# A macaron block (experts, linear attention, experts): attention walked batch by batch, with the norms of the other batch between its units

## What is computed

```python
x = x + 0.5 * _L0_ffn_ref(_layernorm(x), gate_w, Wg, Wu, Wd, cWg, cWu, cWd)
x = x + _L0_attn_ref(_layernorm(x), wq, wk, wv, wo)
x = x + 0.5 * _L0_ffn_ref(_layernorm(x), gate_w, Wg, Wu, Wd, cWg, cWu, cWd)

# attention: q, k rotated (rope); per head, with lam = 2 ** (-8 i / 16):
#   o[i] = sum over j <= i of exp(-lam (i - j)) (q[i] . k[j]) v[j];  result = o @ wo.T
# ffn: logits = x @ gate_w.T; the 4 largest, softmax weights over them;
#   each chosen expert e: down_e(silu(g) * u), plus 0.05 * the chunk expert e // 2
```

## Time and profile before

| | us |
|---|---|
| median of 3 runs | 596.48 (592.13 to 601.65) |
| the profiled execution, its own time | 596.83 |
| its span | 595.1 |
| stage B, from the load of results to the first projection | 153.2 to 181.7 |
| first projections to the first scores | 181.7 to 189.7 |
| stage C, units 0 to 31 | 189.7 to 424.5 |
| stage D to the routing's first matmul | 424.5 to 437.2 |
| routing to the first expert matmul | 437.2 to 458.5 |

### The profile page before, as it was taken

One profiled execution on the slowest core, in us unless ns is written; L12 is line 12 of the kernel. 1 busy time (PEld: TensorE's weight loads), 2 busy tenths in 40 slices (PEclk: granted clock), 3 DMA queues, 4 the chain that ended last, 5 costly groups with the idle time before them and its releaser, 6 DMA issues.

```text
span 595.1 us, 9863 instructions
## 1 busy us (share of the span) xinstructions
PE 507.6 (85%) x3276; PEld 439.8 (74%) x3276; DVE 318.7 (54%) x997; ACT 142.8 (24%) x382; POOL 257.4 (43%) x280
## 2 busy tenths in 40 slices
PE   8589979999039999999999999999858999999900
PEld 7489968887017888889888988888758898888600
DVE  6844333343296647664766476666785444444325
ACT  4102212222234231222132212211420222222211
POOL 0045656663236444434443444333103566666322
PEclk9789999999559999999999999999976999999955
DMA  7989987781650010121012011110295425778173
GB/s 228 322 261 330 331 319 245 257 287 55 236 192 18 28 36 19 54 56 23 31 40 68 19 36 36 52 37 10 86 381 179 154 94 182 234 251 281 55 256 118
DMA packets 46654, 87.79 MB, mean 148 GB/s; under 512 B 6528, under 2 KB 27264, under 8 KB 46592
## 3 DMA queue, kind: packets, MB, share of 16 engines
q1 hardware_dynamic: 37376, 66.05, 34.0%
q0 software_dynamic: 6912, 18.88, 9.4%
q10 hardware_dynamic: 2304, 2.10, 1.0%
HBM read 74.42 MB, written 12.58 MB: 146 GB/s over the span
## 4 chain that ended last, share of the span: by engine, by line
PE 60%; DVE 22%; DMA 11%; issue 3%; SPq 2%; ACT 1%; POOL 1%; POOLq 0%; DVEq 0%; ACTq 0%
PE bank L1180 10%; PE bank L1089 8%; PE bank L1084 7%; PE bank L1217 6%; DMA w_down_sb<-w_down 4%; PE bank L1108 4%; PE bank L1110 4%; PE bank L1193 4%; DVE shared L921 3%; DVE shared L922 3%; DVE shared L920 3%; DMA shared<-z_dram 3%; PE bank L1214 3%; PE bank L1171 3%; PE bank L1199 2%
## 5 line engine op out<-in xcount | busy, mean ns | idle before, releaser
L458 POOL DMA_INDIRECT decay_all<-xn_dram,ids x72 | 69.6, 966 | 121.0 <-PE bank L1056 52.8
L526 POOL TENSOR_TENSOR shared<-shared 128x512 f32<-128x512 f32 x36 | 45.8, 1273 | 130.2 <-DVE shared L922 130.2
L860 DVE COPY oT_all<-bank 128x256 f32<-128x256 f32 x72 | 30.6, 425 | 131.0 <-PE bank L1056 131.0
L467 POOL DMA_INDIRECT z_dram<-probs_all,dest x72 | 70.2, 975 | 36.4 <-ACT probs_all L642 32.7
L1180 PE MATMUL bank<-split_sb 128*128 128x512 f32 x240 | 65.2, 407 | 1.9 <-ACT split_sb L601 0.9
L1089 PE MATMUL bank<-w_ch_sb,oT_all 128*128 128x256 f32 x256 | 65.7, 379 | 0.0
L941 DVE TENSOR_TENSOR split_sb<-bank,split_sb 128x512 fp32r<-128x512 f32 x32 | 22.1, 692 | 66.2 <-ACT split_sb L690 66.2
L634 ACT ACTIVATE rot<-bank 128x224 f32<-128x224 f32 x72 | 25.7, 357 | 132.2 <-PE bank L1089 132.2
L1084 PE MATMUL bank<-w_exp_sb,oT_all 128*128 128x192 f32 x256 | 53.4, 331 | 2.9 <-issue 1.6
L1231 PE MATMUL bank<-split_sb 128*128 128x256 f32 x384 | 53.4, 288 | 1.5 <-DVE split_sb L941 1.5
L1084 PEld LDWEIGHTS bank<-w_exp_sb,oT_all 128*128 128x128 f32 x256 | 43.8, 189 | 10.3 <-issue 5.5
(11 more groups left out here) (141 smaller groups left out, 971.3 us busy)
## 6 DMA issues: line engine op xcount, KB each, us to landing
shared<-w_up_piece SPq DMA_DIRECT2D x32, 448.0 KB, 6.3
w_exp_sb<-w_exp SPq DMA_DIRECT2D x32, 384.0 KB, 8.3
shared<-w_down_piece SPq DMA_DIRECT2D x32, 256.0 KB, 4.3
w_ch_sb<-w_ch SPq DMA_DIRECT2D x16, 384.0 KB, 5.9
shared<-z_dram SPq DMA_DIRECT2D x12, 512.0 KB, 7.1
decay_all<-decay SPq DMA_DIRECT2D x16, 256.0 KB, 2.7
w_down_sb<-w_down SPq DMA_DIRECT2D x16, 192.0 KB, 7.8
xn_dram<-xn_sb ACTq DMA_DIRECT2D x16, 128.0 KB, 6.1
```

The costliest lines, as they stand in the source:

```text
L458: pool.indirect_dma_start(out=xg[s], out_offset=None, in_=xn_dram[l][:, :], in_offset=bass.IndirectOffsetOnAxis(ap=ids[:, SEQ[t]:SEQ[t] + ...
L467: pool.indirect_dma_start(out=z_dram[l][:, :], out_offset=bass.IndirectOffsetOnAxis(ap=dest[:, SEQ[t]:SEQ[t] + 1], axis=0), in_=y_sb[s], i ...
L526: nc.gpsimd.tensor_tensor(dst, rope_a[r % 2], rope_b[r % 2], ALU.add).then_inc(roped, 1)
```

## The change

Attention goes batch by batch: unit n is head n % 16, batch n // 16, so each weight of a head (q, o, decay; k and v of a group) is loaded and split once per batch instead of once for both. The first batch needs only four normalised tiles, so stage B handles tiles 0 to 3. Tiles 4 to 7 are combined on DVE alone (`late_sum`, four chained operations, without ACT and POOL), normalised, transposed and split between units 1 and 11; their residual goes into PSUM in units 12 and 13. In units 17 to 29 the first batch's finished sum is copied out, normalised, transposed, and its logits and top 4 are taken. Stage D then has tiles 4 to 7 alone, and `members` for the first four tiles runs ahead of them.

```diff
-        UNITS, GU = H * B, GROUPS * B
+        UNITS, GS = H * B, HKV * B
         def projections(n, place):
-            g, m = n // GU, n % GU
+            G, m = n // GROUPS, n % GROUPS
             if n < 0:
-                return [("q", 0, 0), ("k", 0, 0), ("v", 0, 0), ("v", 0, 1), ("k", 0, 1), ("t", 0, 0)]
+                return [("v", 0), ("q", 0), ("k", 0), ("t", 0)]
             if place == "scores":
-                return [("q", n + 1, (n + 1) % B)] if n + 1 < UNITS else []
-            if g + 1 < HKV and m >= 2:
-                return [("vvkktt"[m - 2], g + 1, m % 2)]
-            return [("t", 0, 1)] if n == 0 else []
+                return [("q", n + 1)] if n + 1 < UNITS else []
+            return [("vkt"[m - 1], G + 1)] if m >= 1 and G + 1 < GS else []
...
         def splits(n):
             if n < 0:
-                return [("q", 0), ("k", 0)]
-            found = [("o", n // 2)] if n % 2 == 0 else [("q", (n + 3) // 2)] if n + 3 < UNITS else []
-            if n == 0:
-                found.append(("q", 1))
-            if n % GU == 3 and n // GU + 1 < HKV:
-                found.append(("k", n // GU + 1))
+                return [("q", 0), ("k", 0), ("q", 1)]
+            found = [("o", n)]
+            if n + 2 < UNITS:
+                found.append(("q", n + 2))
+            if n % GROUPS == 1 and n // GROUPS + 1 < GS:
+                found.append(("k", n // GROUPS + 1))
...
+        LATE_SUM_AT, LATE_STATS_AT, LATE_NORM_AT, LATE_TURN_AT, LATE_COPY_AT, LATE_RES_AT = 1, 2, 3, 4, 5, 12
+        OUT_AT, STATS_AT, NORM_AT, TURN_AT, COPY_AT, LOGIT_AT, TOP_AT = [H + a for a in (1, 2, 3, 4, 5, 6, 7)]
+        def early_tile(n, first):
+            i = (n - first) // 2
+            return [i] if (n - first) % 2 == 0 and 0 <= i < SB else []
...
+        def load_late(sp, j):
+            if j == 1:
+                sp.wait_ge(xnT_mm, TT + SB)
+            if j >= 2:
+                sp.wait_ge(x_done, SB + j - 1)
+            sp.dma_start(late_z[j % 2], rows_of(0, SB + j)).then_inc(late_z_in[j % 2], 16)
...
+            def load_q(n):
+                if n >= 2:
+                    sp.wait_ge(proj_mm, order.index(("q", n - 2)) + 1)
+                sp.dma_start(wq_sb[n % 2], wq[n % H, :, :]).then_inc(wq_in[n % 2], 16)
+            def load_decay(n):
+                if n >= 2:
+                    sp.wait_ge(masked[1], n - 1)
+                    sp.wait_ge(q_scaled, n - 1)
+                sp.dma_start(decay_sb[n % 2], decay[n % H, :, :]).then_inc(decay_in[n % 2], 16)
+            def load_o(n):
+                if n >= 2:
+                    sp.wait_ge(wo_mm, n - 1)
+                sp.dma_start(wo_sb[n % 2], wo[n % H, :, :]).then_inc(wo_in[n % 2], 16)
+            load_results(sp, 0, SB)
+            load_kv(0)
+            load_q(0)
+            load_q(1)
+            sp.dma_start(cos_sb, cos[:, :]).then_inc(const_in, 16)
+            sp.dma_start(sin_sb, sin[:, :]).then_inc(const_in, 16)
+            load_decay(0)
+            load_o(0)
+            load_decay(1)
+            load_late(sp, 0)
+            load_late(sp, 1)
+            load_q(2)
+            load_kv(1)
...
+            for n in range(UNITS):
+                if n in (2, 4):
+                    load_late(sp, 1 + n // 2)
+                if n + 3 < UNITS:
+                    load_q(n + 3)
+                if n + 1 < UNITS:
+                    load_o(n + 1)
+                if n + 2 < UNITS:
+                    load_decay(n + 2)
+                if n % GROUPS == 3 and n // GROUPS + 2 < GS:
+                    load_kv(n // GROUPS + 2)
...
+            split_rows(pool, 0)
+            split_rows(pool, 1)
+            for key in splits(-1):
+                split_lo(pool, key)
+            split_rows(pool, 2)
+            split_rows(pool, 3)
...
+                for j in early_tile(n, LATE_NORM_AT):
+                    root(act_e, 1, SB + j)
+                for j in early_tile(n, LATE_COPY_AT):
+                    transposed(act_e, 1, SB + j, late_xT_ps[j % 2])
+                for i in early_tile(n, NORM_AT):
+                    root(act_e, 2, i)
+                for i in early_tile(n, COPY_AT):
+                    transposed(act_e, 2, i, early_xT_ps)
...
+                if n in (OUT_AT, OUT_AT + 1):
+                    for i in range(2):
+                        residual_out(2 * (n - OUT_AT) + i)
+            for i in range(SB, TT):
+                residual_out(i)
+            moe_act(act_e, 1)
...
+        def late_sum(dve, link, j):
+            dve.wait_ge(late_z_in[j % 2], 16 * (j // 2 + 1))
+            for k in range(TOP_K):
+                ins = nc.vector.scalar_tensor_tensor(x_sb[:, SB + j, :], late_z[j % 2][:, k, :], wgt[:, SB + j, k:k + 1],
+                                                     x_sb[:, SB + j, :], ALU.mult, ALU.add)
+                if k < TOP_K - 1:
+                    link(ins)
+                else:
+                    ins.then_inc(x_done, 1)
+        def row_stats(dve, link, i, s):
+            if s == 1:
+                dve.wait_ge(x_done, i + 1)
+            if s == 2:
+                dve.wait_ge(x2_copied, i + 1)
+            link(nc.vector.bn_stats(stats[:, i % 2, :], x_sb[:, i, :]))
+            link(nc.vector.bn_aggr(mv[:, i, :], stats[:, i % 2, :]))
+            link(nc.vector.tensor_scalar_add(var_eps[:, i:i + 1], mv[:, i, 1:2], EPS))
+            nc.vector.reciprocal(rvar[:, i:i + 1], var_eps[:, i:i + 1]).then_inc(rvar_ready, 1)
...
+                for j in early_tile(n, LATE_NORM_AT):
+                    normalise(dve, 1, SB + j)
+                for j in early_tile(n, LATE_SUM_AT):
+                    late_sum(dve, link, j)
+                for j in early_tile(n, LATE_STATS_AT):
+                    row_stats(dve, link, SB + j, 1)
+                for i in early_tile(n, STATS_AT):
+                    row_stats(dve, link, i, 2)
+                for i in early_tile(n, NORM_AT):
+                    normalise(dve, 2, i)
+                for i in early_tile(n, TOP_AT):
+                    top_values(dve, 1, i)
+                    top_index(dve, 1, i)
+            split_output(UNITS - 1)
...
-            norm_dve(dve, tick, 1)
-            split_last = attention_dve(dve)
-            norm_dve(dve, tick, 2, split_last)
+            norm_dve(dve, tick, 1, 0, SB)
+            attention_dve(dve, link)
+            members(dve, link, 1, 0, SB)
+            norm_dve(dve, tick, 2, SB)
...
                 if i == 2:
                     residual(0)
-                if i == 4:
+                if i == 3:
                     residual(1)
-                if i == 7:
                     for p in projections(-1, None):
                         project(p)
-            transpose_rows(pe, 1, beside)
+            transpose_rows(pe, 1, beside, 0, SB)
...
+                for j in early_tile(n, LATE_TURN_AT):
+                    if j >= 2:
+                        pe.wait_ge(xnT_copied, TT + SB + j - 1)
+                    transpose_tile(pe, 1, SB + j, late_xT_ps[j % 2])
+                if n in (LATE_RES_AT, LATE_RES_AT + 1):
+                    pe.wait_ge(xnT_copied, 2 * TT)
+                    residual(2 + n - LATE_RES_AT)
+                for i in early_tile(n, TURN_AT):
+                    pe.wait_ge(x2_copied, 2 if i == 0 else SB)
+                    pe.wait_ge(xnT_copied, 2 * TT + i)
+                    transpose_tile(pe, 2, i, early_xT_ps)
+                for i in early_tile(n, LOGIT_AT):
+                    pe.wait_ge(x2_copied, SB)
+                    logits(pe, 1, i)
                 products(n)
```

More of the change, by code:

```diff
@@ L607, in norm_act, with moe_act @@
                     scale_results(act_e, 0, i)
-            for i in range(TT):
+            lag = 2 if s >= 1 else 1
+            for i in range(first, last):
                 n = s * TT + i
-                if s == 1 and i + 3 < TT:
+                if s == 1 and i + 3 < last:
                     scale_results(act_e, 0, i + 3)
-                act_e.wait_ge(rvar_ready, n + 1)
-                nc.scalar.activation(rstd[:, i:i + 1], rvar[:, i:i + 1], ACT.Sqrt).then_inc(rstd_ready, 1)
-                if i == 2 and beside:
-                    beside()
-                lag = 2 if s >= 1 else 1
-                if i >= lag:
-                    transposed(i - lag)
-                if s == 1 and i == TT - 3:
-                    for key in splits(-1):
-                        split_hi(act_e, key)
-            for i in range(TT - lag, TT):
-                transposed(i)
-        def moe_act(act_e, l, beside=None):
-            norm_act(act_e, 2 * l, beside)
+                root(act_e, s, i)
+                if i - lag >= first:
+                    transposed(act_e, s, i - lag, xT_ps[(n - lag) % 2][:, 0:D])
+            if s == 1:
+                for key in splits(-1):
+                    split_hi(act_e, key)
+            for i in range(last - lag, last):
+                transposed(act_e, s, i, xT_ps[(s * TT + i) % 2][:, 0:D])
```

(12 more changed lines are left out.)

325 lines of the change are left out of this document (142 added, 183 removed).

## The result

| | time, us | runs |
|---|---|---|
| kernel before | 596.32 | 4 |
| changed kernel | 608.96 (607.74 to 611.28) | 4 |
| ratio after / before | 1.024 (95% interval 1.018 to 1.031) | |

The interval lies clear of 1, so the kernel is slower; whether by more than 2% it leaves open. The prediction was 598.8 with a range from 590.5 to 605.5. The profiled execution of the changed kernel took 611.28, its span 609.6, against a span of 595.1 before. First the stretches of attention, as windows of the kernel after: length, busy PE, PEld, DVE, ACT, POOL, then granted clock, DMA share and GB/s. They run from the issue of the first load of results to the first scores, to the last output projection, and to the first matmul of the routing.

The account below looks back on a forecast made before the run. DVE's chain was taken to bound stage B, PE attention. Terms -5.6 (stage B), +2.6 (units), +4.6 (PE insertions), +2.6 (DVE insertions), -2.2 (stage D) sum to +2.0 on 596.8: 598.8 us, range 590.5 to 605.5.

Parts of the forecast that it names:

- What bounds the kernel: Whole kernel: DVE's chain sets stage B before attention; PE is full in attention, busy 229.68 of 234.8 us.
- Doubled splitting costs nothing: Units: one more split each on ACT and POOL, about 0.72 us on POOL, ends some 3 us before the next rotation.
- load of results to first q projection: Stage B, before attention: with four tiles the first q projection comes at 176.1, a gain of 5.6 us.
- units (7 v, 7 k, 7 t): Attention units: v and k projections that lay free beside the first rotation now stand in full units, +2.6 us.
- stage D: After attention: fewer normalisations, logits and top 4, and a shorter first comparison start the routing sooner, -2.2 us.
- PE insertions: Units: transposes +1.2, residuals in units 12 and 13 +1.6, logits of four tiles +1.8; sum +4.6 us.
- DVE insertions: Units: statistics +0.6 us, combines of late tiles overrunning the pause in units 3 and 7 +2.0; sum +2.6.
- The rival in which the two exclude each other wholly: Late additions in units: DVE and POOL lock each other out for whole instructions, about +3 us, 601.8; chance 0.08.
- Late decay loads: Units: decay loads come too late for POOL's scaling of q; half a microsecond per unit gives 614 us; chance 0.07.
- PE at 1.2 GHz through v and the first q: Head: the clock stays low, v costs 1.8 us more and q 1.3, giving 601.9; chance 0.15.
- About 244 from the first scores: Sign in the profile after: about 244 us from the first scores to the last unit's end.
- units without insertions last over 6.7: Sign that the prediction is wrong: attention units holding no inserted work take longer than 6.7 us.

Follow-up runs that it names:

- e1: Changed kernel with POOL splitting weights before it adds the rotated q in each unit; 598.51 us, ratio 1.0037 to the kernel before.
- e2: Changed kernel with the q weight's split ahead of the o weight's on ACT and POOL; 600.47 us, ratio 1.0083 to the kernel before.
- e3: Kernel before, with the q weight split in the unit just ahead of its projection, not one unit sooner; 600.27 us, ratio 1.0081.
- e4: e1 with q and k projected ahead of v in the head; 595.46 us, ratio 1.0002 to the kernel before.
- e6: e4 with late additions spread as pairs, the steps behind them moved, residuals in units 13 and 14; 600.2 us, ratio 0.9994 to the kernel before.
- e5: e4 with ten idle matmuls behind the last output projection; 600.82 us, ratio 0.9984 to the kernel before.
- e7: e4 with the edits of e5 and e6, and k projected and rotated ahead of q in the head; 599.29 us, ratio 0.9963 to the kernel before.
- e9: e7 with late tiles' transposes ahead of their unit's projection and residuals in plain units 12 and 16; 592.13 us, ratio 0.9954 to the kernel before.
- e8: e7 with first weights split before the rows of tiles 0 to 3, and residuals behind k, q and v; 594.69 us, ratio 0.9987.

## Why the prediction was wrong, step by step

**What bounds the kernel: right.** With POOL's order mended (e1) time again follows PE's chain: the windows show PE busy for 237.36 of 245.14.

**Doubled splitting costs nothing: this step failed, by 12.5.** The work was sized rightly (rows of 0.73), and so was the slack, but I measured the slack to POOL's own next task, the addition one unit later. The one who waits is PE, for the split weight of its next q projection. The earlier trace rows has POOL's addition at 402.68 and the next rotation at 407.20; the projection between them stands in the same timeline of the kernel before:

```profile
405.52 1.64 PE L1180 MATMUL bank<-split_sb 128*128 128x512 f32 x6
```

Before, the split that this projection needs had been made a unit sooner, so none of POOL's work of this unit stood ahead of it. Now addition, scaling and two splits do. The prediction's own 3.4 for them puts their end at 402.68 + 3.4 = 406.1, already 0.6 late. With what the kernel after shows, 3.45 and 0.25 until PE starts, it is 402.68 + 3.70 = 406.38, which is 0.86 late. That is what the plain units after show (7.52 against 6.68). The step also named the wrong price if the cover went, 22: PE pays only what sticks out, some 0.85, and only in units behind short ones. e1 gives the 12.5 back, e2 shows that it is q's split, and e3 makes the same kind of loss in the kernel before.

With this one step mended the number comes out: e1 took 598.51, where 598.8 was written. That it comes so near is partly luck. Against the kernel before, e1's head gave 7.1 and not 5.6, its stage D 0.2 and not 2.2, and its late work cost 1.2 less, which a unit 0 at a low clock took back. The parts:

| term | predicted | measured |
|---|---|---|
| load of results to first q projection | -5.6 | -6.4 (28.5 to 22.1); to first scores -6.8 |
| units (7 v, 7 k, 7 t) | +2.6 | +2.6 (e4: 8.6 in all, less 6.0) |
| PE and DVE insertions | +7.2 | +6.0 in e4 |
| doubled splitting | 0 | +12.5 |
| low clock in unit 0 | 0 | +1.2 (e1 over e4) |
| stage D | -2.2 | -0.7 after, -0.2 in e1 and e4 |

**PE insertions (+4.6).** The residuals cost 0.48 in unit 12 and 0.86 in 13, 1.3 in place of 1.6. Transposes and logits cost 0.67 in 6, 22 and 26, 0.22 in 10, 0.30 in 24, 0.07 in 28, nothing in 20. With the residuals that is 3.9 in all. Not all of unit 6 is PE's. Unit 10 is a k unit with the same transposes and lost 0.22; in unit 6 PE also waited 0.55 for the rotation behind the late additions, so some 0.4 of it belongs to the next term (an estimate from these two units).

**DVE insertions (+2.6).** The statistics cost nothing in units 2 and 18 (8.07 and 8.08), where I had 0.3 each. The late sums: about 1.8 by e6, where I had 2.0; they showed in units 4 and 8, behind the t units. The pattern that I read in the earlier trace rows, that DVE's additions and POOL's work alternate, is there. The group of tile 4's and 6's additions in the kernel e4, then the timeline of the kernel after in unit 5:

```profile
L749 DVE SCALAR_TENSOR_TENSOR x_sb<-state_sb,wgt,x_sb x8: 479/486/1059, 193.2 to 228.5; 128x256 f32<-128x256 f32 x8
```

```profile
234.33 2.87 DVE L748 SCALAR_TENSOR_TENSOR x_sb<-state_sb,wgt,x_sb 128x256 f32<-128x256 f32 x4
234.96 0.91 POOL L536 TENSOR_TENSOR split_sb<-shared,split_sb 128x256 fp32r<-128x256 f32 x1
```

The numbers behind the colon are the shortest, the median and the longest of eight: 479 ns alone, 1059 when one met POOL. POOL's own row is 0.91 in place of 0.73. Four additions took 3.66, 3.27, 2.87 and 3.62 in the changed kernel, where I had 3.6 for those that meet POOL throughout. The rival in which the two exclude each other wholly would have made it 4.7; no group reached that. (Its price in the time was mis-added: with 4.7, both v units overrun their 3.86 by 0.84 and both t units take 1.1 more, 3.9 in all and not 3.) It rests on the Trainium skill (SBUF — State Buffer, "SBUF: two separate sides"), by which the one of the two that starts first keeps the other out for its whole instruction. This case agrees that they hinder each other, and not over the whole length: beside unit 1's additions POOL's splits started at 200.64, 201.51 and 202.38, so a pair took 0.87, where 0.48 + 0.73 would be 1.21.

**Stage D (-2.2).** Mis-sized by 1.5 in the kernel after and 2.0 in e1 and e4. About 0.9 goes with PE's granted clock (e5 and what followed it: 11.6 on the mean in place of 12.5): PE's rows there are half as long again (0.67 for 0.41, 0.95 for 0.63). With half of the tiles gone PE rests for 2.73 before the first transposes, but e3 shows long rows without such a rest, so what lowers the clock stays open. The rest of the term was not looked into. The clock I had thought of only for the head.

**The rivals.** Late decay loads (614) would have given a number near the result for a wrong reason: in the waits of the kernel after no DMA of a decay stands before POOL's scaling. PE at 1.2 GHz through v and the first q did not come: v took 1.95, and q with k 3.02, where it was 3.01 before. The low clock came later, in unit 0 (8.32 after, 7.97 in e1, 6.77 in e4), and made 1.2 to 1.5.

**What would show it.** "About 244 from the first scores" gave the failure away at once: 257.07. e1 has 245.14 and e4 243.37. So did the sign "units without insertions last over 6.7": they last 7.5. The first q projection (176.86) and the first scores (184.50) came where they were expected.

## What to carry to other kernels

When work is added to an engine with slack, don't compare its sum with the length of a turn. Find the first consumer of each thing that it makes, and add up what now stands ahead of that thing in the engine's order; an engine that idles for 4 us in a turn of 7.5 can still be what everyone waits for. If it idles ahead of a chain and works behind it, try its order first: here that alone, with the same work, gave back the 12.5.

## What was not expected of the hardware

PE's granted clock depended here on more than the length of a rest. In the head, PE rested for 2.57, 2.56 and 2.55 in e4, e5 and e6; unit 0 then took 6.77, 7.45 and 8.34, at granted shares of 1.00, 0.89 and 0.80. With rests of 0.45 and 1.68 (e7) it took 7.61 at 0.87, with 0.46 and 1.67 (e9) 6.68 at 1.00. What tells these apart stays open. In e8 the projections, with nothing ahead of them but transposes and a rest of 1.64, took 4.48 in place of 2.97: the residuals, moved away from PE's slow stretch, left the slowness to them.

A DVE operation on two SBUF inputs was lengthened from 0.48 to at most 1.06 by POOL, and POOL's from 0.73 to 0.91 in the units (0.98 in stage B of e8): both pay, and neither for the whole length of the other.
